# Two transformer layers in a software pipeline: engine orders replaced by newly fitted ones, the weight rests no longer stored

## The reference

```python
# layer 0, per item b
h = layernorm(x) * (1 + ca) + sa
k, q, v = ln(h @ Wk.T), ln(h @ Wq.T), h @ Wv.T        # 16 heads of 16, ln per head
x = x + ga * (softmax(causal(q k^T / 4)) v) @ Wu.T
h = layernorm(x) * (1 + cb) + sb
h = silu(tlin(h, w1)) * tlin(h, w2)                   # 256 -> 1024; weights are -1, 0, 1
h = gelu(tlin(h, h1)); h = gelu(tlin(h, h2))          # 1024 -> 1024, twice
x = x + gb * tlin(h, w3)                              # 1024 -> 256; tlin has one scale per output
# layer 1, per item
xp, z = split(modulated_layernorm(x) @ W_in)          # 512 channels each
dlt, B, C = split(xp @ W_xproj)                       # B, C: 16 states
delta = clip(softplus(dlt @ W_dt + b_dt), 0.001, 0.1)
h_t = (1 + A * delta_t) * h_{t-1} + B_t * delta_t * x_t;  y_t = sum over states of C_t * h_t
x = x + ga * ((y + D * xp) * silu(z)) @ W_out
x = x + gb * (fp6_blocks(modulated_layernorm(x)) @ fp6_blocks(weight).T + bias)
```

## Time and profile before

| | |
|---|---|
| median of 3 runs | 4168.96 us |
| the profiled execution itself | 4167.61 us |
| its span, first to last instruction | 4165.8 us |
| TensorE matmul busy | 3523.9 us (85%) |
| VectorE busy | 3318.2 us (80%) |
| GpSimd busy | 2716.0 us (65%) |
| ScalarE busy | 2583.4 us (62%) |
| mean granted TensorE clock | 0.932 |

### The profile page before, as it was taken

One profiled execution on the slowest core, in us unless ns is written; L12 is line 12 of the kernel. 1 busy time (PEld: TensorE's weight loads), 2 busy tenths in 40 slices (PEclk: granted clock), 3 DMA queues, 4 the chain that ended last, 5 costly groups with the idle time before them and its releaser, 6 DMA issues. The chain is left out here.

```text
span 4165.8 us, 50421 instructions
## 1 busy us (share of the span) xinstructions
PE 3523.9 (85%) x16621; PEld 2034.0 (49%) x16621; DVE 3318.2 (80%) x3646; ACT 2583.4 (62%) x3703; POOL 2716.0 (65%) x1960
## 2 busy tenths in 40 slices
PE   5687888989899998989898898989999898989513
PEld 3263645546373645546373554636364554636201
DVE  4514878989798888979797887979898897979694
ACT  2345566767667676766666676767667676666431
POOL 0132866768595876768595776759586776768563
PEclk9799999999999999999999999999999999999756
DMA  4630201102030301103030211203030211203000
GB/s 164 258 105 15 97 21 62 62 26 97 6 117 1 97 26 61 62 21 102 6 102 17 82 41 46 77 8 115 1 107 16 76 46 41 82 6 102 0 5 5
DMA packets 69435, 247.81 MB, mean 59 GB/s; under 512 B 9472, under 2 KB 10112, under 8 KB 68736
## 3 DMA queue, kind: packets, MB, share of 16 engines
q1 hardware_dynamic: 66816, 235.35, 16.8%
q10 hardware_dynamic: 2304, 8.39, 0.5%
HBM read 212.25 MB, written 31.46 MB: 59 GB/s over the span
## 5 line engine op out<-in xcount | busy, mean ns | idle before, releaser
L671 POOL TENSOR_TENSOR kept<-kept,hb 128x512 f32<-128x512 f32 x640 | 811.0, 1300 | 71.1 <-DVE hb L1925 70.9
L1916 DVE TENSOR_TENSOR_SCAN hb<-ps,hb 128x512 f32<-128x512 f32 x640 | 745.0, 1205 | 17.5 <-ACT ps L1362 12.7
L929 PE MATMUL ps<-hid_bhi,wring 128*128 128x512 f32 x1536 | 628.0, 409 | 70.9 <-issue 53.6
L929 PE MATMUL ps<-hid_blo,wring 128*128 128x512 f32 x1536 | 619.8, 404 | 0.0
L1362 ACT ACTIVATE ps<-kept,a_neg 128x512 f32<-128x512 f32 x640 | 423.0, 690 | 174.4 <-DVE hb L1916 174.4
L929 PE MATMUL ps<-hid_ahi,wring 128*128 128x512 f32 x1280 | 516.7, 404 | 8.0 <-POOL hid_alo L686 8.0
L639 POOL TENSOR_TENSOR kept<-kept,hb 128x1024 f32<-128x1024 f32 x128 | 300.2, 2360 | 336.3 <-DVE hb L1860 297.7
L929 PE MATMUL ps<-hid_alo,wring 128*128 128x512 f32 x1280 | 505.0, 395 | 0.0
L632 POOL TENSOR_SCALAR_AFFINE_SELECT room<-room 128x512 f32<-128x512 f32 x256 | 217.7, 862 | 427.2 <-ACT room L1569 427.2
L1988 DVE TENSOR_REDUCE room<-ps 128x4 f32<-128x2048 f32 (+3 forms) x256 | 375.2, 1486 | 123.6 <-PE ps L1105 111.3
L1925 DVE TENSOR_TENSOR hb<-hb,ps 128x512 f32<-128x512 f32 x640 | 404.0, 673 | 0.1
(11 more groups left out here) (198 smaller groups left out, 7359.2 us busy)
## 6 DMA issues: line engine op xcount, KB each, us to landing
wring<-w_hi SPq DMA_DIRECT2D x352, 512.0 KB, 3.3
kept<-in_wffn SPq DMA_DIRECT2D x22, 512.0 KB, 6.3
w_hi<-wring SPq DMA_DIRECT2D x22, 512.0 KB, 7.0
w_lo<-wrest SPq DMA_DIRECT2D x22, 512.0 KB, 5.2
xn<-in_x_fm SPq DMA_DIRECT2D x17, 512.0 KB, 3.3
out_fm<-xc ACTq DMA_DIRECT2D x16, 512.0 KB, 5.4
room<-in_wmod SPq DMA_DIRECT2D x2, 1536.0 KB, 8.1
win<-in_win SPq DMA_DIRECT2D x1, 1024.0 KB, 8.4
```

Of the source, the lines that this page charges most:

```text
L671: pool.tensor_tensor(acc[:, m, :], acc[:, m, :], hb[:, s % 8, :], ALU.add).then_inc(acc_done, 1)
L929: mm = pe.matmul(bank(bk), wring[:, r % 3, at + k * P:at + (k + 1) * P], src[i][:, k, :], start=(k == 0 and i == 0), stop=(k == K - 1 and ...
L1916: dve.tensor_tensor_scan(hb[:, s % 8, :], bank(2 + m % 2), hb[:, s % 8, :], 0.0, ALU.mult, ALU.add).then_inc(scanned, 1)
```

## The change

All four lists of calls are replaced by other orders of the same calls (the lists of the setup apart, no call is added or taken away). Beside that:

- the rests of the weights are no longer stored: `wrest` and `w_lo` go, `split_dve` writes the rest over the staged tile, and SP stores only `w_hi`. SP stages a tile when the one three before it has been measured, and ScalarE's `split_act` waits for the rest of the tile three before it as well;
- `find_flag` no longer loads the first three tiles; SP does so at the end of the first pass, behind the last store;
- the If in each product is gone. `up` and `mid` have an argument `exact`; the whole feed-forward half of TensorE stands in the program twice, once with raw float32 weights (`wraw`, for weights with rests) and once as before, behind one `pe.If` and `pe.Else`. SP has the same two versions of its loads.

```diff
         def split_sync(sp):
-            for t in range(FT + 2):
+            for t in range(FT + 1):
                 if t < FT:
                     if t >= 3:
-                        sp.wait_ge(w_split, t - 2)
+                        sp.wait_ge(w_measured, t - 2)
                     sp.dma_start(stage[:, t % 3, :], a["wffn"][t]).then_inc(stage_loaded[t % 3], 16)
-                if t >= 2:
-                    r = t - 2
+                if t >= 1:
+                    r = t - 1
                     sp.wait_ge(w_rounded, r + 1)
                     sp.dma_start(w_hi[r], wring[:, r % 3, :].bitcast(F32)).then_inc(hi_stored[r % 3], 16)
-                    sp.wait_ge(w_split, r + 1)
-                    sp.dma_start(w_lo[r], wrest[:, r % 2, :].bitcast(F32)).then_inc(lo_stored[r % 2], 16)
...
-                dve.tensor_tensor(wrest[:, t % 2, :], stage[:, t % 3, :], wring[:, t % 3, :].bitcast(F32), ALU.subtract).then_inc(w_split, 1)
+                dve.tensor_tensor(stage[:, t % 3, :], stage[:, t % 3, :], wring[:, t % 3, :].bitcast(F32), ALU.subtract).then_inc(w_split, 1)
...
-            up(0)
-            up(1)
...
+            def feed_forward(exact):
+                up(0, exact)
+                up(1, exact)
...
+            if ffn:
+                with pe.If(has_rest > 0):
+                    feed_forward(False)
+                with pe.Else():
+                    feed_forward(True)
+            else:
+                feed_forward(True)
...
             exp_probs(3, 1)
+            copy_head(1)
+            exp_probs(3, 2)
             invert_sums(2)
-            fin_rows(1)
-            exp_probs(3, 2)
```

471 lines of the change are left out of this document (230 added, 241 removed).

## The result

| | before | after |
|---|---|---|
| median | 4167.23 us (4 runs, 4163.98 to 4177.01) | 4225.38 us (4 runs, 4218.92 to 4226.48) |
| span of the profiled execution | 4165.8 us | 4223.3 us |
| TensorE matmul busy | 3523.9 us | 3482.0 us |
| mean granted clock | 0.932 | 0.943 |
| written to HBM | 31.46 MB | 19.92 MB |

The account below looks back on a forecast made before the run. TensorE was taken to bound the feed-forward stretch, and a chain across engines the 22 us of the last quads. Gains of 28 (steady passes) + 11 (first pass) + 2 (rest) = 41 us gave 4128 against the median, range 4085 to 4172.

Parts of the forecast that it names:

- The first 94 us have room for both signs: First 94 us of a steady pass: small losses and gains fit in TensorE's 6.1 idle us; 0, bounds -2 and +2.
- (a): Last quads: scores_turned(3, 0) starts earlier, with values(2, 0) moved ahead of turn_max(3); 0.9 us gained a pass.
- (b): Last quads: exp_probs(3, 2) no longer stands behind invert_sums(2) and fin_rows(1); 0.7 us gained, bounds 0 and 0.77.
- the forecast had 0.3 there: Ahead of the last layer norm's square: copy_b(2), standing behind invert_sums(3), makes it late; 0.3 us lost a pass.
- The clock: At att_proj(0) and up(0): shorter waits keep matmuls off the lower clock level; 0.7 us gained a pass, bounds 0 and 3.4.
- rival C: At the last quads and up(0): both clock falls go, 3.4 instead of 0.7 us a pass, 4090 us; chance 17%.
- Rival A: Steady passes keep their length, early losses (exp_probs(2, 1), pick_mod) cancel (a) and (b), first pass gains: 4158 us; chance 19%.
- Rival B: At up(0): TensorE's long jump shows, 4.3 us in each of 15 feed-forward halves, 4192 us; chance 14%.
- The first pass: First pass: one of three tile transfers goes; 11 us gained, at most 17, or nothing if the attention's chain takes over.
- The same bytes per second would need 63 us: First pass: with one of three transfers gone, DMA at the same 349 GB/s would take 63 us instead of 94.
- The rest: The pass without fin and the two that empty the pipeline: 2 us gained, bounds +8 and -10.
- VectorE against GpSimd: Long scans beside GpSimd's on-chip reads, 2505 ns mean against 2284 median, 1.8 us a pass: nothing counted of it.

Follow-up runs that it names:

- s1: Changed kernel with three tiles staged ahead and the old order in the first 94 us of a pass, new order behind: 4138.85 us, ratio 0.9938.
- e3: Changed kernel with one edit in SP's staging, three tiles loaded before the first store, new lists kept: 4224.68 us, ratio 1.0147.
- e4: Changed kernel with the four old lists of calls and three tiles staged ahead; rests still unstored, long jump kept: 4160.9 us, ratio 0.9996.
- s9: Changed kernel with three tiles staged ahead, new order only in the first 94 us of a pass, old order behind: 4254.81 us, ratio 1.0216.
- g2: e4 with in_proj(3) moved ahead of scores_turned(0, 2) on TensorE and copy_xp(1) ahead of exp_probs(0, 2) on ScalarE: 4205.76 us, ratio 1.0095.
- g3: e4 with two VectorE moves, normalise(3) ahead of tail_out(0, 0) and find_max(0, 2) behind tail_out(0, 1): 4165.19 us, ratio 1.0006.
- b2: b1 with both att_add moved ahead of head_scan(1, 0) and ffn_centre ahead of head_out(1, 0) on VectorE: 4114.05 us, ratio 0.9882.
- e1: Changed kernel with the four old lists of calls; its new staging and long jump kept: 4168.28 us, ratio 0.9997.
- e2: Kernel before with the four new lists; its old staging and an If in each product kept: 4225.56 us, ratio 1.0142.
- p1: e3 with ScalarE's split(4, 5, 6) back ahead of exp_probs(0, 0) and split(7, 8, 9) right behind it: 4214.55 us, one execution.
- s7: s1 with the feed-forward half's lists old as well, so new order only from fin_turn(0) to up(0): 4144.24 us, ratio 0.995.
- b1: s1 with pick_mod on VectorE moved from ahead of find_max(0, 0) to behind find_max(1, 0) and tail_in(1, 0): 4150.66 us, ratio 0.9966.
- g1: Changed kernel, three tiles staged ahead, old order in a pass's first 28 us, in_proj(3) behind turn_max(1), copy_xp(3) behind exp_probs(0, 2): 4220.89 us, ratio 1.012.

## Why the prediction was wrong

**The step that failed** is "The first 94 us have room for both signs (6.1 us of idle TensorE); I take 0 for them, bounds -2 (gain) and +2". It measured 4.8 us lost at `fin_turn(0)`, with the clock at 1.00 in both, and 4.0 to 4.7 a pass in the mean of 12 (s1 to e3, e4 to s9). The cover did not exist. TensorE's 6.1 us are small waits (the longest sum, 2.0, is for exponentials), and idle time of an engine does not cover a delay of the chain that runs from the maximum of a quad to its turned scores, to the exponential and to the next `turn_max`. I had looked there only at the edits that seemed small (`pick_mod`, `exp_probs(2, 1)`) and not at the two that stand on that chain, `find_max(0, 2)` behind two `tail_out` and `in_proj(3)` ahead of `scores_turned(0, 2)`. Alone, the second delays the chain by 1.7 us (g2; 3.5 a pass and 45 in all with the clock that then falls), the first by 1.7 as well, of which 1.4 are left at the last layer norm (g3). Either is within the +2 that I had given to all together; with 3.4 they make up most of the 4.8, and the rest isn't isolated by a run.

The step was one of several. A quiet pass, term by term (us, + is longer; "at clock 1.00" compares after with passes of the old lists in which the clock is up: before from 778.3 on, e4 from 1240.0 on for the last half):

| | forecast | measured |
|---|---|---|
| first 94 us, to `fin_turn(0)` | 0 (-2 to +2) | +4.8 |
| (a) and (b), to `att_proj(0)`, at clock 1.00 | -1.6 | -0.6 |
| to the mean of the last layer norm, at clock 1.00 | +0.3 | +1.1 |
| to `up(0)` | 0 | +0.1 |
| lists of the feed-forward half, at clock 1.00 | 0 | -0.3 |
| the clock | -0.7 (0 to -3.4) | -5.6 |
| sum | -2.0 | -0.5 |

Over the whole kernel 41 us gained were forecast and 58 lost were measured. Of these 99 us, 46 are in the steady passes, 32 in the first one and 20 in the rest.

**(b) was right, (a) mis-sized.** (b) measured 0.70 as forecast. For (a) the time from `exp_probs(2, 2)` to `exp_probs(3, 0)` fell from 6.21 to 4.04 us, but in the pass of the kernel before with its clock up it is 4.16: the order gave 0.1, not 0.9. Of the 1.07 us read from the earlier trace rows, 0.43 are left when the matmuls of `values(2, 0)` run at full clock. And behind `att_proj(0)` the new order loses 1.1 us to the scan beside `head_times(1)` that b2 moves; the forecast had 0.3 there, for another reason. "I take the 14 steady passes as alike" hid all this: they run from 232.2 to 235.7 us (245.2 at the loop's turn) by the clock.

**The clock** did what rival C wanted in the quiet passes: 3.4 us at the lower level in the attention half, where before had 13.7, and none at `up(0)` (3.4 before). `att_proj(0)` went from 3.52 to 1.99. That is worth 4.1 us up to the last layer norm and 1.5 behind `up(0)`, more than the bound. In the mean of 12 passes it gave less: 15.1 us at the lower level in before, 5.1 in after. That a quiet pass came out 0.5 us shorter, with the sign of the forecast, is luck: a gain of the clock that was taken at an eighth of its size covered a loss that was taken as zero.

**Rival A** had the closest mechanism (early losses cancel (a) and (b); quiet passes 235.0 against 235.6) and the wrong place: `pick_mod` takes no part in the loss, and `exp_probs(2, 1)` costs 0.7 us (it is 5.5 us late, `exp_probs(2, 0)` 4.8) that `fin_turn(0)` doesn't see. The sign that the prediction gave for being wrong, a pass as long as before although (a) and (b) are there, is what came. **Rival B** is refuted by e1 (95.1 us, 3.47 idle) and by the rows of `up(0)`: what the Trainium skill says of a taken branch's fetch (Runtime: NRT & Kernel Launch, section "Instruction fetch mechanics") may hold, but no run here shows a wait of TensorE for it. The 5.1 us at the loop's turn would then be the barriers and the clearing for the larger part; this wasn't measured by itself. Rival B's price was also counted for 15 feed-forward halves; there are 16, one for each item, and at 4.3 us each it would have been 69 us and not 64.

**The first pass.** I took 11 us gained, bounds 0 and 17; the staging gave 4.6 to 5.5 (e1, e4), and the new lists took 21 in the new staging (e4 to e3) and 17 in the old (before to e2, 246.5 to 263.3). "The same bytes per second would need 63 us" was wrong. In e4, over the same 94 us:

```profile
80.00:174.00 94.00, 57.54 (x378) 25.07 (x376) 78.09 (x67) 45.73 (x47) 8.63 (x11) 0.66 0.75 246
...
ACT wring L439 <- DMA kept<-in_wffn: 33.4, 17, 3.1
```

The DMA engines are 0.75 busy at 246 GB/s, and ScalarE still waits 33.4 us for tiles: not the bytes set the pace, but, as far as the rows tell, each tile's own chain of load, rounding and measuring with three places to lie in. In after ScalarE waits for `scores_turned` instead:

```profile
ACT room L1565 <- PE ps L1118: 29.8, 4, 11.6
ACT wring L439 <- DMA kept<-in_wffn: 18.6, 7, 4.5
```

The sentence "nothing goes if the attention's chain, interleaved by the fixed order, takes over" named the mechanism and stopped at zero. In e3 the roundings stand behind an exponential that waits 11.6 us, and undoing two such places gave 5.7 us back (p1); for the rest of the 21 it is argued, not shown.

**The rest.** 2 us gained, bounds +8 and -10, measured 17 to 18 lost, all of it in the pass without `fin`. Three terms are seen there: the lists of the first 94 us (the attention half of s9 takes 144.9 us, of e1 138.2: 6.7), those of the feed-forward half (101.2 in e1, 103.7 in s1: 2.5), and the clock, 47 us at the lower level instead of 26. e1 and e4, with the same lists and another staging in the pass before, differ by 8.7 us in this pass with 45.8 and 25.8 us at the lower level, so no order of this pass was shown to set this term.

**VectorE against GpSimd.** I counted nothing. The long scans went from 2505 to 2635 ns in the mean and GpSimd's `tail_add`, before always 2332 to 2385, to a mean of 3025:

```profile
L625 POOL TENSOR_TENSOR kept<-kept,hb 128x1024 f32<-128x1024 f32 x128 | 385.8, 3025 | 210.2 <-DVE hb L1856 189.5 <-issue 20.7
L1849 DVE TENSOR_TENSOR_SCAN hb<-hb 128x1024 f32<-128x1024 f32 x128 | 337.2, 2635 | 6.9 <-POOL hb L682 2.8 <-ACT hb L1333 0.2
```

In b2 `tail_add` is back at 2360 ns. Of two instructions of 2.3 us the one that starts second takes 4.3 (the scan of s1 at 3467.87), and a multiplication of 128x2 values takes 2.32 (s1) where it takes 0.16 in e4. The Trainium skill (SBUF — State Buffer, section "SBUF: two separate sides") has this as an exclusive lock, held by whichever starts first for its whole instruction; these rows agree. What it costs depends on who stands behind: 1.6 us at `att_add`, 1.7 at `find_max(0, 0)`.

## What to carry to other kernels

A list of calls that is read against one stretch must be read against all: follow the one chain that runs through the whole pass, and price each call that was put ahead of one of its links at its full length, also where the engine shows idle time (here 1.7 us for a call of 1.8, and 1.7 for two of 0.7 and 1.2). A small instruction can take as long as the one that runs beside it on another engine: 2.32 us for 128x2 values here. And before a gain of one or two microseconds a pass is believed or given up, look at whether the clock fell at the same place in both traces. Here the trace of the kernel before had passes of each kind: the rows for a step can be taken from one with the clock up, and what the clock costs from the difference.

## What the runs showed of the hardware

- The same program has passes that differ by up to 4 us, by where TensorE's granted clock goes to its lower level (0.5, 1.2 GHz). Before mostly loses it at 96, 113 and 140 us of a pass; e4, with the same lists, has two passes of 231.7 us that lose it only for 3.4 us at 99 and at 130. The idle times of TensorE just ahead of it (1.07 and 1.51 us, before its work at 94 and 97 us) are the same in before, e4, s1, b2 and s7, in passes with the fall and without, so they alone do not decide it.
- Between 94 and 102 us of a pass the clock falls in 10 of 13 passes of before and of e4, 13 of e1, 4 of s7 and of b2, 11 of b1 and none of s1 and of after. The late order has a part in that, and so has the moment at which the late part starts: a shift of the early part by 1.7 us (g3) brought it from 10 to 4 (and one at 104), one of 1.3 us the other way (s1 to b1) from none to 11.
- A long jump of TensorE, over the whole second version of the feed-forward half, cost nothing that a trace shows: that half takes 95.1 us in e1 and in before, and 93.6 in passes of both with the clock up.
- The profiled execution of g1 was granted 0.899 in the mean, where its relatives have 0.94, and took 4251.6 us against 4211.57 to 4226.08 for its other three. For 3502 of its 4250 us the record shows 0.949, a value that no other trace here has. No lengths of passes are taken from it.
